# A graph layer on one core: the type check, the bias of x, the weight scales and the next normalises move to other engines and places

## What is computed

```
h    = max(layernorm(x), 0)
hi_t = h @ W1[:384] + emb[adj] @ W1[384:] + b1      # per pair i, j
hj_t = h @ W2[:384] + emb[adj] @ W2[384:] + b2
A    = softmax(where(adj != 0, sum(hi_t * hj_t, -1), -1e9), axis=2)
out  = x + relu((A @ h) @ gcn_w + gcn_b) @ Wo + bo
```

## Time and profile before

| what | value |
|---|---|
| median of 3 runs | 383.42 us (381.75, 383.42, 383.49) |
| the profiled execution | 383.2 us |
| its span | 381.3 us |
| PE busy | 361.4 us (95%) |
| DVE busy | 268.4 us (70%) |
| ACT busy | 270.2 us (71%) |
| POOL busy | 192.0 us (50%) |
| mean granted clock of PE | 0.982 |

### The profile page before, as it was taken

How to read it: one execution, slowest core, us unless ns; L and a number is a source line. 1 busy time by engine, 2 the same in 40 slices (tenths; PEclk the granted TensorE clock), 3 DMA queues, 4 the chain that set the end, 5 groups by cost and what they waited for, 6 DMA issues and landing times.

```text
span 381.3 us, 9507 instructions
## 1 busy us (share of the span) xinstructions
PE 361.4 (95%) x3150; PEld 227.6 (60%) x3150; DVE 268.4 (70%) x663; ACT 270.2 (71%) x572; POOL 192.0 (50%) x353
## 2 busy tenths in 40 slices
PE   8998495799999999999999999999999999999986
PEld 8674263556566665656575756666565657575654
DVE  1779388758677777859595867777776949567674
ACT  3546368197887878787969788787878786974733
POOL 2089868028282836565473728283746556390000
PEclk9999889699999999999999999999999999999999
DMA  7961420556383947655565748393755644444143
GB/s 232 345 190 74 92 79 2 112 168 135 85 249 83 239 91 194 134 172 119 158 145 136 180 96 234 83 247 83 219 111 181 125 121 92 140 89 130 37 117 134
DMA packets 82216, 53.88 MB, mean 141 GB/s; under 512 B 45666, under 2 KB 82148, under 8 KB 82196
## 3 DMA queue, kind: packets, MB, share of 16 engines
q1 hardware_dynamic: 81488, 53.22, 53.7%
q0 software_dynamic: 64, 0.20, 0.3%
q10 hardware_dynamic: 644, 0.20, 0.2%
HBM read 17.44 MB, written 12.58 MB: 79 GB/s over the span
## 4 chain that ended last, share of the span: by engine, by line
PE 85%; POOL 5%; DVE 4%; ACT 2%; issue 2%; DVEq 0%; ACTq 0%; POOLq 0%
PE bank L1105 23%; PE bank L1106 22%; PE bank L1107 22%; PE bank L1199 6%; POOL x_all L392 3%; PE bank L1350 3%; PE bank L1345 3%; PE bank L1117 2%; DVE h_parts L1040 1%; PE bank L1149 1%; PE bank L1316 1%; POOL root_sq L346 1%; ACT h_tok L490 1%; PE bank L1140 1%; PE bank L1415 1%
## 5 line engine op out<-in xcount | busy, mean ns | idle before, releaser
L428 POOL TENSOR_TENSOR h_parts<-h_tok,h_parts 128x1536 f16<-128x1536 f32 (+1 forms) x14 | 42.0, 2999 | 98.1 <-ACT h_parts L481 98.1
L1105 PE MATMUL bank<-gw_hi,hT 128*128 128x385 f16 x192 | 63.6, 331 | 7.6 <-DVE hg_lo L771 6.4
L1107 PE MATMUL bank<-gw_hi,hT 128*128 128x385 f16 x192 | 63.3, 330 | 0.0
L1106 PE MATMUL bank<-gw_lo,hT 128*128 128x385 f16 x192 | 63.2, 329 | 0.0
L1105 PE MATMUL bank<-wo_hi,z_hi 128*128 128x384 f16 x180 | 58.8, 327 | 0.0
L1106 PE MATMUL bank<-wo_lo,z_hi 128*128 128x384 f16 x180 | 58.7, 326 | 0.0
L1107 PE MATMUL bank<-wo_hi,z_lo 128*128 128x384 f16 x180 | 58.7, 326 | 0.0
L434 POOL TENSOR_TENSOR x_all<-x_all,bo_all 128x1536 f32 (+1 forms) x16 | 55.2, 3453 | 0.0
L1105 PE MATMUL bank<-hT,m_hi 128*128 128x512 f16 x144 | 54.8, 381 | 0.0
L1106 PE MATMUL bank<-hT,m_hi 128*128 128x512 f16 x144 | 54.7, 380 | 0.0
L1107 PE MATMUL bank<-hT,m_lo 128*128 128x512 f16 x144 | 54.6, 379 | 0.0
(11 more groups left out here) (161 smaller groups left out, 695.7 us busy)
## 6 DMA issues: line engine op xcount, KB each, us to landing
x_all<-in_x_dram SPq DMA_DIRECT2D x16, 768.0 KB, 6.2
out_dram<-x_all SPq DMA_DIRECT2D x15, 768.0 KB, 4.0
hg_parts<-hg_lo SPq DMA_DIRECT2D x32, 192.0 KB, 3.3
hg_parts<-hg_hi SPq DMA_DIRECT2D x32, 192.0 KB, 3.6
x_all<-in_L_gnn_W_w_dram SPq DMA_DIRECT2D x2, 576.0 KB, 5.1
out_dram<-x_all SPq DMA_DIRECT2D x4, 192.0 KB, 1.9
gcn_raw<-in_L_gnn_gcn_w_dram SPq DMA_DIRECT2D x1, 576.0 KB, 10.7
x_all<-in_L_gnn_Wo_w_dram SPq DMA_DIRECT2D x1, 576.0 KB, 11.3
```

The source lines that it names most:

```text
L428: nc.gpsimd.tensor_tensor(h_parts[:, tiles, 1, :], h_tok[:, tiles, :], h_parts[:, tiles, 0, :], ALU.subtract).then_inc(h_split, 1)
L1105: nc.tensor.matmul(dst, lh, rh, start=(c == 0), stop=False)
L1106: nc.tensor.matmul(dst, lh, rl, start=False, stop=False)
L1107: last = nc.tensor.matmul(dst, ll, rh, start=False, stop=(c == DC - 1))
```

## The change

Five edits, all ahead of the loop over the supertiles.

1. The type check: ACT sums max(adj/2 - 1/2, 0) of each quarter of `adj` with an accumulator (`types_above`, four activations), between the high parts of h(0) and those of gw. PE adds the four sums by one matmul 1x4 behind hg(0,0), in place of the eight. DVE reduces four numbers and writes `has_types` before it is through with hg(0,2) and hg(0,3). POOL's four pieces go.
2. POOL adds `bo` to x(0) right after h(0) is normalised; before, it did so after the low part of h(2). Then come the coefficients of h(1), then a wait for h(1), then `make_bias`.
3. The norms behind the gcn and output scales: PE's two transposes come ahead of the pair matmuls and its spread of the maximum right behind h(0)'s transposes; DVE works out the scales before G(0), one BN_STATS of x(1) at a time between the dependent steps, with x(2)'s statistics moved ahead of the low parts of G(0). `gw_hi` comes ahead of all of G(0)'s parts. The output weights are split in three pieces; their low parts lie between h(1)'s low parts and behind the first masking.
4. h(1) is normalised by ACT (tiles 0, 1) and DVE (tiles 2, 3).
5. The shared normalise of h(2) is cut in two: `shared_high_parts` ahead of `attention_high(1)`, `shared_low_parts` behind the low part of G(1)'s last chunk.

The core of the diff:

```diff
-                nc.gpsimd.memset(const_all[:, n, :], value)
-            ins = nc.gpsimd.memset(ones16[:, :], 1.0)
+                ins = nc.gpsimd.memset(const_all[:, n, :], value)
...
-            def types_excess(n):
...
-                piece = adj_all.rearrange("p t j -> p (t j)")[:, n * QUARTER:(n + 1) * QUARTER]
-                nc.gpsimd.tensor_scalar(excess[n], piece, -float(EDGE), 0.0, ALU.add, ALU.max).then_inc(type_excess, 1)
...
-                pool.wait_ge(type_excess, 2 * n + 2)
+                pool.wait_ge(type_sums, 2 * n + 2)
...
-            pool.wait_ge(h_ready, 2 * KT)
-            pool.wait_ge(adj_loaded, 16)
-            types_excess(0)
-            types_excess(1)
-            pool.wait_ge(weight_scales_ready, 1)
-            pool.wait_ge(adj_rest_loaded, 16)
-            types_excess(2)
-            types_excess(3)
+            def add_bias(s):
...
+                pool.wait_ge(h_ready, 2 * KT * (s + 1))
+                nc.gpsimd.tensor_tensor(x_all[:, s, :, :], x_all[:, s, :, :],
+                                        bo_all[:, :, :].broadcast_to([P, KT, D]),
+                                        ALU.add).then_inc(x_biased, 1)
...
+            pool.wait_ge(bo_loaded, 16)
+            add_bias(0)
...
+            pool.wait_ge(h_ready, 2 * KT * 2)
...
-            add_bias(0)
...
+            def types_above(n):
...
+                act.wait_ge(adj_loaded if n < 2 else adj_rest_loaded, 16)
+                piece = adj_all.rearrange("p t j -> p (t j)")[:, n * QUARTER:(n + 1) * QUARTER]
+                nc.scalar.activation(type_scratch[n], piece, ACT.Relu, bias=const_all[:, 2, 0:1], scale=0.5 / EDGE,
+                                     accum_out=type_sum[:, n:n + 1]).then_inc(type_sums, 1)
...
+            def wo_high_part(c):
...
+                act.wait_ge(wo_scale_ready, 1)
+                nc.scalar.activation(wo_hi[:, c, :], wo_raw[:, c, :], ACT.Copy,
+                                     scale=scale[:, SC_WO:SC_WO + 1]).then_inc(wo_high, 1)
...
-            act.wait_ge(pair_bias_made, 1)
-            g_high_part(0, 0)
-            g_whole(0)
+            act.wait_ge(consts_made, 1)
+            for n in range(4):
+                types_above(n)
...
-            for c in range(1, DC):
+            act.wait_ge(pair_bias_made, 1)
+            for c in range(DC):
...
-            act.wait_ge(wo_scale_ready, 1)
-            nc.scalar.activation(wo_hi[:, :, :], wo_raw[:, :, :], ACT.Copy,
-                                 scale=scale[:, SC_WO:SC_WO + 1]).then_inc(wo_high, 1)
-            for k in range(1, KT):
-                hg_high_part(0, k)
-            early_normalise(1, range(KT))
+            wo_high_part(0)
+            hg_high_part(0, 1)
+            early_normalise(1, range(0, EARLY_WIDE))
+            hg_high_part(0, 2)
+            wo_high_part(1)
+            wo_high_part(2)
+            hg_high_part(0, 3)
...
+            def second_statistics(tiles):
...
+                dve.wait_ge(x1_loaded, 16)
+                dve.wait_ge(coef_ready, COEF_STEPS)
+                for k in tiles:
+                    ins = nc.vector.bn_stats(stats6[:, k, :], x_all[:, 1, k, :])
+                if tiles[-1] == KT - 1:
+                    ins.then_inc(stats_ready, 1)
...
+            def early_normalise(s, tiles):
+                dve.wait_ge(coef_ready, COEF_STEPS * (s + 1))
+                if s:
...
+                    dve.wait_ge(early_t, DC * s)
+                for k in tiles:
+                    nc.vector.tensor_scalar(h_tok[:, k, :], x_all[:, s, k, :], ln_mul[:, k:k + 1], ln_add[:, k:k + 1],
+                                            ALU.mult, ALU.add).then_inc(h_ready, 2)
...
+            early_normalise(0, range(EARLY_WIDE))
...
+            nc.vector.tensor_reduce(norm_top[:, :], bank[6][0:1, NORM_ROWS].rearrange("p (n q) -> p n q", n=2),
...
+            nc.vector.tensor_scalar(peak[:, SC_WO:SC_GCN + 1], bank[6][:, NORM_WIDE], TINY, None,
+                                    ALU.max).then_inc(scale_step, 1)
+            second_statistics(range(0, 1))
+            peak_exponent(SC_WO, SC_GCN + 1, 5)
...
+            scale_from_exponent(SC_WO, SC_GCN + 1, 5)
...
+            scale_ready(SC_WO, SC_GCN + 1, 5, scale_step)
+            second_statistics(range(1, 2))
+            dve.wait_ge(scale_step, 9)
+            nc.vector.tensor_scalar(gcn_bias[:, :], gcn_raw[:, :, D], scale[:, SC_GCN:SC_GCN + 1], Y_SCALE,
...
+            second_statistics(range(2, KT))
...
+            def wo_low_part(c):
+                dve.wait_ge(wo_high, c + 1)
+                low_part(wo_lo[:, c, :], wo_raw[:, c, :], wo_hi[:, c, :], SC_WO).then_inc(wo_split, 1)
...
+            statistics(2)
...
-            dve.wait_ge(wo_high, 1)
-            low_part(wo_lo[:, :, :], wo_raw[:, :, :], wo_hi[:, :, :], SC_WO).then_inc(wo_split, 1)
+            dve.wait_ge(type_row, 1)
+            nc.vector.tensor_reduce(type_top[:, :], bank[7][0:1, 0:4], AX.X, ALU.max).then_inc(type_step, 1)
...
-            rows_and_low(0, 2)
-            statistics(2)
-            rows_and_low(0, DC)
-            dve.wait_ge(type_row, 1)
-            nc.vector.tensor_reduce(type_top[:, :], bank[7][0:1, :], AX.X, ALU.max).then_inc(type_step, 1)
...
+            early_normalise(1, range(EARLY_WIDE, KT))
+            rows_and_low(0, 2)
+            rows_and_low(0, DC)
...
+            def shared_low_parts(s):
...
-                for c in range(DC):
-                    early_low_part(1, c)
+                early_low_part(1, 0)
+                wo_low_part(0)
+                early_low_part(1, 1)
+                wo_low_part(1)
+                early_low_part(1, 2)
...
+                wo_low_part(2)
...
+                third_mean_made()
...
-                third_mean_made()
+                shared_high_parts(2)
...
-                shared_normalise(2)
+                shared_low_parts(2)
...
+            pe.wait_ge(norm_made, 2)
+            for n in range(2):
+                last = nc.tensor.transpose(bank[6][0:1, n * P:(n + 1) * P], norm_part[:, n:n + 1], ident[:, :])
+            last.then_inc(norm_rows, 1)
...
+            pe.wait_ge(norms_top, 1)
+            nc.tensor.matmul(bank[6][:, NORM_WIDE], ones[0:1, :], norm_top[0:1, :], start=True,
+                             stop=True).then_inc(norms_wide, 1)
...
-                if c == 0:
-                    pe.wait_ge(norms_top, 1)
-                    nc.tensor.matmul(bank[6][:, NORM_WIDE], ones[0:1, :], norm_top[0:1, :], start=True,
-                                     stop=True).then_inc(norms_wide, 1)
...
-            pe.wait_ge(consts_made, 1)
-            pe.wait_ge(pairs_copied, 2)
-            for n in range(4):
-                pe.wait_ge(type_excess, n + 1)
-                for piece in range(0, QUARTER, 512):
...
-                    last = nc.tensor.matmul(bank[7][0:1, :], ones16[:, :], tops, start=(n == 0 and piece == 0),
...
-            last.then_inc(type_row, 1)
...
-            hg_read(KT)
+                if k == 0:
...
+                    pe.wait_ge(type_sums, 4)
+                    pe.wait_ge(pairs_copied, 2)
+                    nc.tensor.matmul(bank[7][0:1, 0:4], ones[:, 0:1], type_sum[:, :], start=True,
+                                     stop=True).then_inc(type_row, 1)
...
+                hg_read(KT)
...
-                pe.wait_ge(wo_split, 1)
+                pe.wait_ge(wo_split, DC)
```

47 lines of the change are left out of this document (11 added, 36 removed).

## The result

The changed kernel takes **366.75 us**, the median of four runs (366.61 to 367.03), against 382.97 (381.75 to 383.49) before: a ratio of 0.958, interval 0.956 to 0.961. The forecast was 367.0. The profiled execution has a span of 364.9 for 381.3, which is 16.4 less, the sum of the forecast. What follows asks whether it came about in the way that was forecast.

A forecast was written before the change was run, and what follows sets the result against it. PE, busy 95%, was bound by waits of 6.4 and 5.62 us ahead of the loop and half clock behind them. Terms sum to -16.4: 383.2 becomes 366.8, plus 0.2 for the median, 367.0 us; range 364.5 to 371.5.

The forecast's parts named there:

- Up to hg(0), -1.4: Ahead of hg(0): ACT's sums, 1.05 each, and earlier scales let gw_lo be ready, removing PE's 1.20 wait and 0.2: -1.4 us.
- the type matmuls, -1.7: On PE behind hg(0): eight type matmuls, 1.96 us with their tail, become one, counted at 0.2: -1.7 us.
- The rival in which the sums block ACT: Ahead of hg(0): ACT's third sum waits for a late second half of adj, delaying gw_hi and everything else; chance 0.02.
- The first hole, -4.6: PE's idle time of 5.6 us ahead of h(1)'s transposes becomes 1.0, for PE's branch; they start at 37.2: -4.6 us.
- The rival of a dear branch: Ahead of h(1)'s transposes: PE's branch takes all of 4.4 us and the clock falls as before, giving 373.2; chance 0.09.
- The new waits, +0.5, +1.4, +0.3, +0.65, and 0.35 at hg(1,3): New PE waits: h(1)'s low parts +0.5, hg(1,0) +1.4, next chunk's low part +0.3, attT_hi +0.65; 0.35 left at hg(1,3).
- The clock, -2.8 and -2.7: PE's clock stays full behind both former long idle times, since no wait lasts 4.6 us: -2.8 and -2.7 us.
- The second hole, -6.1: PE's 6.4 us wait ahead of hg(1,3) becomes 0.35, add_bias(0) being long done and DVE's two L1040 taking 0.9: -6.1 us.
- The lock: DVE against POOL: by the trace row a late make_bias would not hold wo_lo; by the skill's rule, some 1 us more.

The follow-up runs named there:

- run 8: The changed kernel with PE waiting, ahead of the transposes of h(1), for one or three small transfers: 369.13 us (one), 372.52 us (three).
- run 3: The kernel before with the type check on ScalarE, make_bias behind h(1), types read earlier and h(1) normalised earlier: 383.15 us, ratio 1.002.
- run 2: The kernel before with only the type check moved to ScalarE, the rest in its old order: 382.78 us, ratio 1.001.
- run 7: The changed kernel without PE's branch for edge types above 1: 366.56 us.
- run 4: The kernel of run 3 with an unused tile dropped, hg_read(KT) behind PE's branch and x(2)'s statistics ahead of G(0)'s low parts: 371.28 us, ratio 0.972.
- Run 1: The kernel before without POOL's addition of the output bias to x(0): 377.16 us, ratio 0.988.
- run 5: The changed kernel with the bias of x(0) at its old place, behind token_low(2): 367.23 us.
- 6: The changed kernel without POOL's wait for h(1) ahead of make_bias: 367.45 us.

## Why the prediction was right

The time was right, and so were most terms of the sum and the path by which they work. Three things in it were not: the first hole was sized 1.0 too small, with something given back behind it; the reason for a full clock did not hold as a rule; and the cause of the second hole's end was only half of it.

- *Up to hg(0), -1.4, and the type matmuls, -1.7.* hg(0,0) starts at 30.00, so 1.6; one sum takes ACT 1.13 from start to start, for 1.05 assumed; the types' matmul is 0.19, and from hg(0,0) to the end of that work PE needs 6.1 for 7.95. Right. That the third sum starts just as its data lands was right too (24.08, 0.4 behind the landing), and thinner than I priced it. The rival in which the sums block ACT had a chance of 0.02; a landing some 3 us later, as four of the runs have it, makes it real at about 2 us (hg(0,0) at 31.9 for 30.0 in run 8).
- *The first hole, -4.6.* It went altogether (5.6 to 0), and the transposes came at 36.13 for the 37.2 foretold. I had put 1.0 for the branch of PE behind h(1). The branch does cost: 1.45 and 1.6 us when PE stands at it (runs 3 and 2). But the types are known at 34.63 and the matmuls already queued last until 36.1, so it is over by then. Some of it comes back as 0.48 inside the scores, a term that the sum did not have, where it only takes the place of waits for `hT` (run 7); the rest is lost at hg(1,0), whose time DVE sets. That is why an error of 1.0 left no trace in the total. The rival of a dear branch is out.
- *The new waits, +0.5, +1.4, +0.3, +0.65, and 0.35 at hg(1,3).* They are 0.45, 1.37, 0.19, 0.29 and 0.33, so only the fourth, for `attT_hi`, was sized twice too long. The chain of DVE, worked out from its rows, was the best part of the forecast: hg(1,0) was foretold for 47.7 and came at 47.65, hg(1,3) for 55.2 and came at 55.00.
- *The clock, -2.8 and -2.7.* It is full throughout. But the reason given, that no wait lasts as long as the 4.6 behind which it fell, was not safe. Idle times of 2.2 us (ahead of hg(0,0) in run 8, with three transfers), 2.76 (run 4) and 3.03 (run 8) brought it down, to half for 3.4 us each; those of 1.37, 1.7 and 1.9 us left it full, and so did the 3.27 us of run 1. So the length of the idle time does not decide by itself, and what else does is open: no run varies one hole and leaves the rest as it was. Run 1 had its expected full clock, but not for the reason given there either. In the kernel before I had read when the clock fell, not how little can be enough. With waits of at most 1.37 us the changed kernel stays below every idle time that brought the clock down here.
- *The second hole, -6.1.* It went, and both L1062 ran free. That it goes *because the bias of x(0) is added early* is half of the cause. Run 1 shows the cause in the old order. In the new one DVE reaches L1062 at 50.4, 4 us ahead of POOL's next pass, and the old place of the bias costs 0.5 (run 5). PE's wait at hg(1,3) is 0.32 there, as in the changed kernel, so in this order the early bias is not what closes the hole, and the order of run 4, with the bias where it was, took 4.5 of its 6.4. The sum had the right total and would have had the wrong shares.
- *The lock.* Here I went by the row and not by the rule, and the rule was right where it mattered. Runs 2 and 6 show POOL's `make_bias`, with one SBUF input, holding DVE's two-input `wo_lo` (2.95 for 1.42) and even the two one-input instructions that normalise h(1) (3.33 for 0.85). In the kernel after, the first `wo_lo` takes 0.75 for 0.60, which fits `make_bias` ending at 39.4. The Trainium skill (SBUF — State Buffer, section "Who interferes with whom") states both: two SBUF inputs contend with a GpSimd instruction that reads SBUF, and `tensor_scalar` can take both port pairs. The trace agrees with it in these three places, and disagrees for the type pieces of the kernel before, beside which `gw_lo` ran unhindered. Why those differ was not tried. It cost the forecast 0.15 us, and it is what POOL's new wait for h(1) is for.

Part of the total is luck: the terms are off by up to 1.0 either way and cancel (16.7 at the output of supertile 0, for 16.4 foretold).

The parts alone: part 1 with its order takes 10.5 off (run 4), leaving out the bias of x(0) in the old order 4.8 (run 1), all five edits together 16.2. The early scales of edit 3 were not tried alone. The type check alone is worth nothing (run 2): it frees POOL, and the next in line, DVE's reading of the types and PE's wait ahead of its branch, then holds the hole open.

Not settled: why `adj_all` lands later in the four kernels. Run 4 differs from run 3 in two other places, both on compute engines and later than the issue of the transfer, so the address is the likely cause, not one isolated by itself. It need not be the address of `adj_all` alone: `x_all` moves by the same bytes, and in the first 40 us the same 5792 packets of SP's queue take 70.3% of the 16 DMA engines' time in run 3, for 59.0% in run 4. The Trainium skill (DMA: Bandwidth & Descriptors, section "Specifications") gives 512 B as the least size for full rate. The Trainium skill (DMA: Bandwidth & Descriptors, section "How a descriptor splits into AXI transactions") states that a descriptor which does not start at a multiple of 256 bytes gets a first transaction from the boundary below it, at the price of extra beats. The direction agrees with the later landing here; no trace shows the transactions, and no run moved one of the two tiles by itself.

## What to carry to other kernels

Removing the first of several causes of a wait gives only what the next one allows: list who would hold it next, and test a part together with what it needs, or it will look worthless. Two holes in a row share their causes, so price them in order, not one by one. And after adding or dropping even a small tile, look at where the large ones begin and at the landing times of their transfers before reading anything into a time.

## What the hardware showed that was not expected

- The same transfer of `adj_all` (256 bytes per row) landed 13.1 to 15.3 us after issue in ten kernels where the tile begins at a multiple of 256 bytes, and 16.3 to 18.8 in four where it and `x_all` are 32 or 64 off.
- PE, standing at a branch on a loaded value, went on 1.6 us after the value was written (run 2), and 1.45 us after the wait just ahead of the branch had ended (run 3). With matmuls queued for as long, leaving the branch out made no difference that can be told (366.56 for 366.75).
- An idle time of 2.2 us brought PE to half its clock for 3.4 us, and one of 3.27 us did not: its length alone does not tell.
- Two DVE `tensor_scalar` with one SBUF input each were held by a POOL pass with one SBUF input: 3.33 us for 0.85.
